# Causal attention on Trainium2: the first scores in a ring of three single PSUM banks, the second scores in a ring of three, and row maxima over one bank

## The chip, the core and the metric

The kernel runs on one NeuronCore of one Trainium2 chip. The metric is the device time in microseconds (us) of one launch of the whole program.

The engines are named as in the profile: PE is TensorE (matmuls; PEld are its weight loads, which overlap them), DVE is VectorE, ACT is ScalarE, POOL is GpSimd, SP is SyncE. The matmul results land in PSUM, which has eight banks of 512 float32 values per partition.

## The reference

The program is a chain of eight layers (four attention-like mixers, four feed-forward ones) over 32 batches of 256 tokens with 128 features. The change touches one of them, the third mixer, a causal attention with 16 heads of 8 features. After low-rank projections it computes, for each batch and head:

```
scores = q @ k.T / sqrt(8)            # 256 x 256, masked to columns <= row
attn   = softmax(scores, axis=-1)
o      = attn @ v                     # 256 x 8
x      = x + concat(o over heads) @ W_o
```

A second attention near the end of the program (no mask, called `h3`) shares its code with this one (`h2`).

## The kernel before

`attend(tag, causal, ...)` emits both attentions. The work goes batch by batch. For a batch the kernel makes two sorts of score:

- **First scores** (queries on partitions), only to find each row's maximum. `late_scores` does the rows 128 to 255 of two heads into one bank (2 matmuls of 256 columns and a mask matmul of 256 columns; L2312, L2314). `early_scores` does the rows 0 to 127 of four heads into one bank (4 of 128 columns and a mask matmul of 512; L2327, L2329). Two banks make a *unit*. A batch has six units, and DVE's `maximum` (L2198) reduces a unit in one instruction of 1024 elements per partition. `ps_1` has four banks, so it holds two units; unit k uses banks 2*(k%2) and the next one.
- **Second scores** (keys on partitions), with the negated maxima as extra rows of q. `scores` does one head into one bank of `ps_2` (256 + 128 columns and a mask matmul of 256; L2355, L2356, L2358). ACT's `weights` (L2449) takes the exponential of the bank into SBUF. `ps_2` has two banks, head h uses bank h%2.

After four heads `weigh` (L2377) multiplies the exponentials with the values: 16 matmuls that use a 128x32 tile of the array each, four side by side. `turn_sums`, `turn_max`, `turn_out` and `project_out` (L2386, L2392, L2399, L2406) turn the sums, the maxima and the output, all through one bank `ps_m`; DVE's `norm` and `added` (L2205, L2209, L2216) and ACT's copies (L2454, L2466, L2472) stand between them. POOL splits the maxima of a batch in three bfloat16 parts (L2244 to L2250) and sends them by DMA into the extra rows of q (L2275).

Everything is software pipelined and the order on each engine is written out by hand in `step`. In step b, PE does for h = 0 to 15: the second scores of head h of batch b, now and then one of the helpers, and then in twelve of the sixteen places (h%8 in 0, 1, 3, 4, 5, 7) one bank of first scores of batch b+2 (`max_scores`). Steps -2 and -1 have first scores alone, steps 30 and 31 second scores alone, and step 32 finishes the last batch. The loop covers the steps 1 to 28.

Buffers are freed by counts. `at(name, b, k)` is "signal `name` has been raised k times in batch b", so `at("ex", b, -1)` means all but the last of the sixteen exponentials of batch b-1. Two waits matter here, both on PE:

```
pe.wait_ge(*at("mx", b, k - 1))       # unit k of first scores: unit k-2 has been reduced
pe.wait_ge(*at("ex", b, h - 1))       # head h of second scores: head h-2 has been exponentiated
```

The second one holds across batches as well: 16 is a multiple of two, so head 0 uses the bank of head 14 before it, and head 1 that of head 15.

Of the kernel before, what the change touches and what calls it, by code (L numbers as in the profile page):

```python
# [19 lines left out]
P = 128  # L20
# [152 lines left out]
def build(nc, x_in, pack_in, maskb_in, w0_in, w1_in, w3_in, out, ktab, ychan, q_stack, k_stack, ones_rows, v_ones,  # L173
          m_parts, xs1, xs3, ys):
    ctx = ExitStack()
    with ctx:
# [11 lines left out]
        def bank(name, stack, n=1):  # L188
            return stack.enter_context(nc.psum_tensor(name, [P, n, 512], F32))
# [99 lines left out]
        for t, nf, choices in (("e1", F1 // P, 2), ("e3", F3 // P, 1)):  # L289
# [25 lines left out]
                ("s1", units), ("mx", units), ("mf", 1), ("ms", 3), ("ml", 1), ("mt", 1), ("mc", 1),   # L315
                ("vp", 2), ("s2", NH), ("ex", NH), ("pv", 4), ("ev", 2), ("tu", 2), ("rec", 2), ("on", 2), ("ot", 1),
                ("otc", 1), ("out", 1), ("x", 1))},
            loaded=[SlotSignal(pool, f"{t}_loaded{u}", 64, u + 4, 4) for u in range(4)]) for t, units in (("h2", 6), ("h3", 8))}
        z_s, z_n, z_g, z_a = sig("z_shifted", 1), sig("z_normed", 1), sig("z_gain", 1), sig("z_done", 1)
        z_d = [SlotSignal(pool, f"z_stored{j}", 16, j, 6) for j in range(6)]  # L320

# [1776 lines left out]
        def attend(tag, causal, dst, w, buffers, load):  # L2098
# [2 lines left out]
            scale = HD ** -0.5  # L2101
            SW = SEQ + P if causal else TPB * SEQ
            UNITS = s["mx"].per

            def at(name, b, k):

                return s[name].now(b, k)
# [6 lines left out]
            with ExitStack() as st:  # L2114
# [11 lines left out]
                oT = sb(f"{tag}_oT", [P, SEQ], stack=st)  # L2126
                identb = sb(f"{tag}_identb", [P, P], BF16, stack=st)
                zero = sb(f"{tag}_zero", [P, 1], stack=st)
                ps_1 = bank(f"{tag}_ps_1", st, 4)
                ps_2 = bank(f"{tag}_ps_2", st, 2)  # L2130
                ps_of = bank(f"{tag}_ps_o", st)
                ps_mf = bank(f"{tag}_ps_m", st)
                ps_o, ps_m = ps_of[:, 0, 0:SEQ], ps_mf[:, 0, 0:SEQ]
# [21 lines left out]
                with pool.loop_block(NB) as block:  # L2155
# [19 lines left out]
                    @block.vector  # L2175
                    def _(dve):
                        for n in range(2):
                            link(dve, dve.memset(vp[n][:, :, :, :], 0.0))
                        link(dve, dve.memset(zero[:, :], 0.0))
                        link(dve, dve.tensor_copy(identb[:, :], ident))  # L2180

                        def maximum(b, u, k):

                            n = u % 2
                            dve.wait_ge(*at("s1", b, k + 1))
                            if k == 0:
                                dve.wait_ge(*at("ml", b, -1))
                            pair = ps_1[:, 2 * (k % 2):2 * (k % 2) + 2, :]
                            if not causal:
                                to, got = nm[n][:, 2 * k:2 * k + 2, :], pair.rearrange("p o (q c) -> p o q c", q=TPB)  # L2190
                            elif k % 3 != 1:
                                h0 = 8 * (k // 3) + HG * (k % 3 // 2)
                                to = nm[n][:, h0:h0 + HG, 1].rearrange("p (o h) -> p o h", o=2)
                                got = pair.rearrange("p o (h c) -> p o h c", c=SEQ)
                            else:
                                to = nm[n][:, 8 * (k // 3):8 * (k // 3) + 8, 0].rearrange("p (o h) -> p o h", o=2)
                                got = pair.rearrange("p o (h c) -> p o h c", c=P)
                            dve.tensor_reduce(to, got, AX, ALU.max, negate=True).then_inc(s["mx"].sem, 1)  # L2198

                        def norm(b, k):  # L2200

                            tv = ps_m.rearrange("p (q h e) -> p q h e", q=TPB, e=16)
                            dve.wait_ge(*at("tu", b, k + 1))
                            dve.wait_ge(*at("on", b, k))
                            dve.reciprocal(rec[:, :, :], tv[:, :, :, HD]).then_inc(s["rec"].sem, 1)  # L2205
                            dve.wait_ge(*at("rec", b, k + 1))
                            if k == 0:
                                dve.wait_ge(*at("ot", b, 0))
                            dve.tensor_tensor(on[:, :, 8 * k:8 * (k + 1), :], tv[:, :, :, 0:HD],  # L2209
                                              rec[:, :, :].unsqueeze(3).to_broadcast([P, TPB, 8, HD]), ALU.mult  # L2210
                                              ).then_inc(s["on"].sem, 1)

                        def added(b):
                            dve.wait_ge(*at("out", b, 1))
                            xd = dst[:, ds(b * TPB, TPB), :]
                            dve.tensor_tensor(xd, xd, ps_m.rearrange("p (t d) -> p t d", t=TPB), ALU.add  # L2216
                                              ).then_inc(s["x"].sem, 1)

                        def step(b, u, r, first, turn, body, tail):
                            for k in range(UNITS):  # L2220
                                if k == 1 and tail:
                                    norm(b - 1, 0)
                                if k == (3 if causal else 4) and tail:
                                    norm(b - 1, 1)
                                if k == UNITS - 1 and tail:
                                    added(b - 1)
                                if first:
                                    maximum(b + 2, u, k)
                            if tail:
                                count(dve, dst, (b - 1) * TPB, TPB, *at("x", b - 1, 1))  # L2230

                        run(dve, step)
# [48 lines left out]
                    def _(pe):  # L2281
# [3 lines left out]
                        def unit_free(b, u, r, k):  # L2285

                            if k == 0 and isinstance(b, int) and b < SLOTS:
                                pe.wait_ge(first_in[tag][u], 48)
                                if b == 2:
                                    pe.wait_ge(first_in[tag][3], 48)  # L2290
                            elif k == 0:
                                pe.wait_ge(*s["loaded"][u].last(r, 64))
                            pe.wait_ge(*at("mx", b, k - 1))

                        def pair_scores(b, u, r, k):

# [6 lines left out]

                        def late_scores(b, u, r, half, part, bank):

                            k = 3 * half + 2 * part
                            if bank == 0:
                                unit_free(b, u, r, k)
                            o = ps_1[:, 2 * (k % 2) + bank, :].rearrange("p (h c) -> p h c", c=SEQ)
                            for j in range(2):  # L2310
                                h = 8 * half + HG * part + 2 * bank + j
                                pe.matmul(o[:, j, :], sq[u][:, h, P:2 * P], sk[u][:, h, :], start=(j == 0), stop=False,  # L2312
                                          skip_group_check=True)
                            ins = pe.matmul(o[:, :, P:2 * P], mskb[:, 0:P], mskb[:, P:2 * P].unsqueeze(1).to_broadcast([P, 2, P]),  # L2314
                                            start=False, stop=True, skip_group_check=True)
                            if bank == 1:
                                ins.then_inc(s["s1"].sem, 1)

                        def early_scores(b, u, r, half, bank):

                            k = 3 * half + 1
                            if bank == 0:
                                unit_free(b, u, r, k)
                            o = ps_1[:, 2 * (k % 2) + bank, :].rearrange("p (h c) -> p h c", c=P)
                            for j in range(HG):
                                h = 8 * half + HG * bank + j
                                pe.matmul(o[:, j, :], sq[u][:, h, 0:P], sk[u][:, h, 0:P], start=(j == 0), stop=False,  # L2327
                                          skip_group_check=True)
                            ins = pe.matmul(o[:, :, :], mskb[:, 0:P], mskb[:, P:2 * P].unsqueeze(1).to_broadcast([P, HG, P]),  # L2329
                                            start=False, stop=True, skip_group_check=True)  # L2330
                            if bank == 1:
                                ins.then_inc(s["s1"].sem, 1)

                        def max_scores(b, u, r, h):

# [12 lines left out]
                        def scores(b, u, h):  # L2348

                            if h == 0:  # L2350
                                maxima_moved(pe, b)
                            pe.wait_ge(*at("ex", b, h - 1))
                            o, hd = ps_2[:, h % 2, :], head(h)
                            if causal:
                                pe.matmul(o[:, 0:SEQ], sk[u][:, hd, 0:P], sq[u][:, hd, :], start=True, stop=False, skip_group_check=True)  # L2355
                                pe.matmul(o[:, SEQ:SW], sk[u][:, hd, P:2 * P], sq[u][:, hd, P:], start=False, stop=False,  # L2356
# [86 lines left out]
                    def _(act):  # L2443
                        def weights(b, h):
                            g, j = h // HG, h % HG
                            act.wait_ge(*at("s2", b, h + 1))
                            if j == 0:
                                act.wait_ge(*at("pv", b, g - 1))
                            act.activation(pt[g % 2][:, j, :], ps_2[:, h % 2, 0:SW], ACT.Exp, scale=scale).then_inc(s["ex"].sem, 1)  # L2449

                        def keep_sums(b, k):
                            act.wait_ge(*at("pv", b, 2 * k + 2))
# [526 lines left out]
```

## Time and profile before

| what | value |
|---|---|
| median of three runs | 3539.38 us (3533.64 to 3543.10) |
| profiled execution, its own time | 3545.52 us |
| span of the profile (first to last instruction) | 3543.7 us |
| mean granted PE clock over the span | 0.863 |
| causal attention stage, from its first reduction's set-up to its last statistics | 1882.5 to 2343.0 us, 460.5 us |
| PE busy in that stage | 452.39 us |
| DVE, ACT, POOL busy in that stage | 287.45, 283.68, 103.34 us |

The profiled execution stands 6.1 us above the median. The stage is 13% of the span. A busy PE in this profile is a PE with a matmul in its pipeline, since the ends of matmuls are modelled; start times tell more: a matmul of 256 columns at full clock is followed by the next one 0.11 us later.

### The profile page before, as it was taken

To read this page: it belongs to the slowest core of one execution; us is meant where nothing else is said; L and a number is where in the kernel's file an instruction comes from. 1 tells how busy PE (TensorE), PEld (TensorE's weight loads), DVE (VectorE), ACT (ScalarE), POOL (GpSimd) and SP (SyncE) were. 2 spreads that over 40 slices of the span, in tenths; PEclk is the share of its full clock that TensorE was granted. 3 is DMA by queue.
4 is the path that set the end of the run, shared out by engine and by line. 5 is a ranking of instruction groups with operands and counts; after the bars stand their busy time and mean duration, and the time that the engine had idled before them with its cause. 6 is when DMAs were issued, how large, how long until landed. Compare 5 with 4: busy or idle time off the path is not lost. (4 is left out here: it accounts for less than half of the span.)

```text
span 3543.7 us, 71949 instructions
## 1 busy us (share of the span) xinstructions
PE 2592.4 (73%) x20194; PEld 1890.8 (53%) x20194; DVE 2241.5 (63%) x4945; ACT 1578.9 (45%) x3615; POOL 725.9 (20%) x1065
## 2 busy tenths in 40 slices
PE   3545858999977666999157999986564999982280
PEld 1333453449966532999135777765332666652260
DVE  5924967238778522676765666646885888865267
ACT  2503612334354232666043666642243777751253
POOL 0000100000000166455301222200221222212553
PEclk7878959999999588999588999978798999985695
DMA  3097100100090111222396555500077565610123
GB/s 95 5 256 178 59 0 14 36 22 0 0 157 26 45 43 43 69 69 65 122 317 75 67 73 72 67 1 1 0 244 149 71 74 72 73 42 20 53 78 101
DMA packets 337603, 261.80 MB, mean 74 GB/s; under 512 B 24988, under 2 KB 319308, under 8 KB 337164
## 3 DMA queue, kind: packets, MB, share of 16 engines
q1 hardware_dynamic: 309720, 223.88, 31.1%
q0 software_dynamic: 19072, 28.28, 2.6%
q10 hardware_dynamic: 8704, 8.39, 0.8%
q8 instruction: 46, 0.75, 0.1%
q14 instruction: 61, 0.50, 0.1%
HBM read 144.03 MB, written 113.29 MB: 73 GB/s over the span
## 5 line engine op out<-in xcount | busy, mean ns | idle before, releaser
L2449 ACT ACTIVATE h_pt<-h_ps 128x384 f32<-128x384 f32 (+1 forms) x1024 | 543.0, 544 | 279.0 <-PE h_ps L2358 143.8
L2198 DVE TENSOR_REDUCE h_nm<-h_ps 128x4 f32<-128x1024 f32 (+1 forms) x448 | 538.9, 1218 | 159.9 <-PE h_ps L2329 64.1
L1607 POOL DMA_INDIRECT sorted_rows<-e_row,e_pos x192 | 184.6, 961 | 439.9 <-DVE e_row L1586 236.1
L1797 POOL DMA_INDIRECT results<-e_y,e_ykey x208 | 211.5, 1017 | 193.4 <-DVE e_y L1786 174.0
L2377 PE MATMUL h_ps_o<-h_pt,h_vp 128*32 128x256 f32 (+1 forms) x4096 | 246.8, 359 | 1.3 <-ACT h_pt L2449 1.3
L1844 ACT ACTIVATE e_hid<-e_ps_h,e_wt 128x128 f32<-128x128 f32 x688 | 202.4, 368 | 20.6 <-PE e_ps_h L1818 14.1
L1818 PE MATMUL e_ps_h<-e_hT,e_wt 128*128 128x128 f32 x1376 | 198.7, 284 | 16.0 <-ACT e_hT L1839 8.2
L1754 DVE TENSOR_SCALAR e_wt<-w 128x1156 f32 (+1 forms) x208 | 139.8, 673 | 98.9 <-DVE e_y L1786 68.9
L2363 PE MATMUL h_ps<-h_sq,h_sk 128*128 128x256 bf16 x1024 | 193.6, 275 | 9.2 <-ACT h_pt L2449 4.4
L1826 PE MATMUL e_ps_o<-e_wt,e_hid 128*128 128x128 f32 x1376 | 195.3, 281 | 4.9 <-ACT e_hid L1844 1.8
L1818 PEld LDWEIGHTS e_ps_h<-e_hT,e_wt 128*128 128x128 f32 x1376 | 175.0, 196 | 29.2 <-issue 17.6
L2300 PE MATMUL h_ps<-h_sk,h_sq 128*128 128x256 bf16 x1024 | 154.9, 275 | 41.6 <-DVE h_identb L2180 34.4
L1826 PEld LDWEIGHTS e_ps_o<-e_wt,e_hid 128*128 128x128 f32 x1376 | 173.1, 194 | 8.7 <-issue 5.4
L2377 PEld LDWEIGHTS h_ps_o<-h_pt,h_vp 128*32 128x32 f32 x4096 | 107.1, 109 | 92.3 <-issue 36.7
L2244 POOL TENSOR_TENSOR h_mpart<-h_nm,h_zero 128x32 bf16<-128x32 f32 x64 | 14.9, 233 | 674.5 <-DVE h_nm L2198 674.5
L1811 PE MATMUL e_ps_t<-pack,e_xt 128*128 128x128 f32 x208 | 58.6, 284 | 121.4 <-DMA e_xt<-sorted_rows 121.2
L2355 PE MATMUL h_ps<-h_sq,h_sk 128*128 128x256 bf16 x512 | 140.5, 274 | 2.1 <-ACT h_pt L2449 1.7
L2358 PE MATMUL h_ps<-h_mskb 128*128 128x256 bf16 x512 | 139.6, 273 | 0.0
L1141 DVE TENSOR_TENSOR x_hid<-x_gelu,x_ps_u 128x512 f32<-128x512 f32 x64 | 43.3, 687 | 141.9 <-ACT x_gelu L1126 141.9
L2312 PE MATMUL h_ps<-h_sk,h_sq 128*128 128x256 bf16 x512 | 99.3, 277 | 45.6 <-DVE h_identb L2180 44.5
L2300 PEld LDWEIGHTS h_ps<-h_sk,h_sq 128*128 128x128 bf16 x1024 | 99.1, 98 | 57.4 <-DVE h_identb L2180 34.6
L2363 PEld LDWEIGHTS h_ps<-h_sq,h_sk 128*128 128x128 bf16 x1024 | 83.7, 98 | 71.7 <-ACT h_pt L2449 62.0
(436 smaller groups left out, 6261.0 us busy)
## 6 DMA issues: line engine op xcount, KB each, us to landing
h_sq<-q_stack SPq DMA_DIRECT2D x64, 384.0 KB
h_sk<-k_stack SPq DMA_DIRECT2D x64, 384.0 KB
sorted_rows<-pad SPq DMA_DIRECT2D x26, 520.0 KB, 10.7
e_xt<-sorted_rows SPq DMA_DIRECT2D x104, 130.0 KB
e_got<-results SPq DMA_DIRECT2D x24, 512.0 KB, 6.3
q_stack<-p_parts SPq DMA_DIRECT2D x32, 384.0 KB
k_stack<-p_parts SPq DMA_DIRECT2D x32, 384.0 KB
v_ones<-p_v SPq DMA_DIRECT2D x32, 288.0 KB, 2.7
```

What stands on the lines that cost most here:

```text
L1607: gp.indirect_dma_start(xs[:, :], bass.IndirectOffsetOnAxis(ap=pos[:, n % choices, tile:tile + 1], axis=0), row[n % ROWS][:, :], None).the ...
L1754: dve.tensor_scalar(wt[j % 4][:, :], w[:, :, :].rearrange("p e w -> p (e w)")[:, ds(at, wc)], 1.0, None, ALU.mult).then_inc(e_w.sem, 1)
L1797: gp.indirect_dma_start(ys[:, :], bass.IndirectOffsetOnAxis(ap=key[m // 4][:, m % 4:m % 4 + 1], axis=0), y[m][:, :], None).then_inc(return ...
L1818: pe.matmul(ps_h[:, k, 0:P], wt[j % 4][:, f * P:(f + 1) * P], hT[j % 4][:, :], start=True, stop=True).then_inc(e_h.sem, 1)
L1826: ins = pe.matmul(o, hid_t[m][:, f, :], wt[m][:, f_dim + f * D:f_dim + (f + 1) * D], start=(f == 0), stop=(f == nf - 1))
L1844: act.activation(hid_t[j % 4][:, f, :], ps_h[:, (j * nf + f) % 4, 0:P], func, bias=wt[j % 4][:, o_b1 + f:o_b1 + f + 1]).then_inc(e_a.sem, 1)
L2198: dve.tensor_reduce(to, got, AX, ALU.max, negate=True).then_inc(s["mx"].sem, 1)
L2300: ins = pe.matmul(ps_1[:, h % 4, q * SEQ:(q + 1) * SEQ], sq[u][:, h, q * P:(q + 1) * P], sk[u][:, h, :], start=True, stop=True)
L2355: pe.matmul(o[:, 0:SEQ], sk[u][:, hd, 0:P], sq[u][:, hd, :], start=True, stop=False, skip_group_check=True)
L2363: ins = pe.matmul(o[:, t * SEQ:(t + 1) * SEQ], sk[u][:, hd, t * P:(t + 1) * P], sq[u][:, hd, :], start=True, stop=True)
L2377: ins = pe.matmul(ps_o[32 * j:32 * (j + 1), q0:], vp[u % 2][:, t, head(HG * g + j), :], pt[g % 2][:, j, t * SEQ:(t + 1) * SEQ - q0], start ...
L2449: act.activation(pt[g % 2][:, j, :], ps_2[:, h % 2, 0:SW], ACT.Exp, scale=scale).then_inc(s["ex"].sem, 1)
```

## The change

The causal attention gets other rings. (The attention without a mask keeps its four and two banks and its waits.)

- `ps_1` becomes a ring of three single banks. A unit is now one bank: twelve units in a batch, each with its own wait and its own signal. Unit k waits until unit k-3 has been reduced.
- DVE reduces each bank by itself: twelve instructions of 512 elements in place of six of 1024. `norm` and `added` stand at the same places between them.
- `ps_2` becomes a ring of three banks, head h uses bank h%3. Head h waits until head h-3 has been exponentiated. As 16 is not a multiple of three, the first three heads of a batch have counts of their own: head 0 falls on the bank of head 15 of the batch before (15%3 = 0), head 1 on that of head 13, head 2 on that of head 14.

```
+            RING = 3 if causal else 2
...
-                ps_1 = bank(f"{tag}_ps_1", st, 4)
-                ps_2 = bank(f"{tag}_ps_2", st, 2)
+                ps_1 = bank(f"{tag}_ps_1", st, 3 if causal else 4)
+                ps_2 = bank(f"{tag}_ps_2", st, RING)
...
# DVE, maximum
-            elif k % 3 != 1:
-                h0 = 8 * (k // 3) + HG * (k % 3 // 2)
-                to = nm[n][:, h0:h0 + HG, 1].rearrange("p (o h) -> p o h", o=2)
-                got = pair.rearrange("p o (h c) -> p o h c", c=SEQ)
             else:
-                to = nm[n][:, 8 * (k // 3):8 * (k // 3) + 8, 0].rearrange("p (o h) -> p o h", o=2)
-                got = pair.rearrange("p o (h c) -> p o h c", c=P)
+                half, i = divmod(k, UNITS // 2)
+                part, o = divmod(i, 2)
+                if part != 1:
+                    h0, n_h, q = 8 * half + HG * (part // 2) + 2 * o, 2, 1
+                else:
+                    h0, n_h, q = 8 * half + HG * o, HG, 0
+                to, got = nm[n][:, h0:h0 + n_h, q], ps_1[:, k % RING, :].rearrange("p (h c) -> p h c", h=n_h)
             dve.tensor_reduce(to, got, AX, ALU.max, negate=True).then_inc(s["mx"].sem, 1)
...
# DVE, step: the same places among twice as many units
-                                if k == 1 and tail:
+                                if k == (2 if causal else 1) and tail:
                                     norm(b - 1, 0)
-                                if k == (3 if causal else 4) and tail:
+                                if k == (6 if causal else 4) and tail:
                                     norm(b - 1, 1)
...
# PE, unit_free
-                            pe.wait_ge(*at("mx", b, k - 1))
+                            pe.wait_ge(*at("mx", b, k + 1 - RING))
...
# PE, late_scores (early_scores alike)
-                            k = 3 * half + 2 * part
-                            if bank == 0:
-                                unit_free(b, u, r, k)
-                            o = ps_1[:, 2 * (k % 2) + bank, :].rearrange("p (h c) -> p h c", c=SEQ)
+                            k = 6 * half + 4 * part + bank
+                            unit_free(b, u, r, k)
+                            o = ps_1[:, k % RING, :].rearrange("p (h c) -> p h c", c=SEQ)
...
# PE, scores
-                            pe.wait_ge(*at("ex", b, h - 1))
-                            o, hd = ps_2[:, h % 2, :], head(h)
+                            pe.wait_ge(*at("ex", b, h + 1 - RING if h >= RING or not causal else (0, -2, -1)[h]))
+                            o, hd = ps_2[:, h % RING, :], head(h)
```

The order of the matmuls on PE stays as it was; what moves is where PE waits. Here is PE at the seam between two batches, before the change: head 15 of batch b (L2355 to L2358), a bank of first scores (L2312, L2314), and head 0 of batch b+1. `signal20` counts exponentials, `signal9` reduced units.

```order
L2355 MATMUL h_ps<-h_sq,h_sk 128x256 [waits signal20]
L2356 MATMUL h_ps<-h_sq,h_sk 128x128
L2358 MATMUL h_ps<-h_mskb 128x2x128
L2312 MATMUL h_ps<-h_sk,h_sq 128x256 x2
L2314 MATMUL h_ps<-h_mskb 128x2x128
L2149 ISA
L2352 ISA [waits h2_maxima_in]
L2355 MATMUL h_ps<-h_sq,h_sk 128x256 [waits signal20]
```

The same place in the changed kernel (L2351 to L2354 are the second scores there, L2313 and L2315 the first):

```order
L2351 MATMUL h_ps<-h_sq,h_sk 128x256 [waits signal20]
L2352 MATMUL h_ps<-h_sq,h_sk 128x128
L2354 MATMUL h_ps<-h_mskb 128x2x128
L2295 REGISTER_ALU
L2313 MATMUL h_ps<-h_sk,h_sq 128x256 [waits signal9]
L2313 MATMUL h_ps<-h_sk,h_sq 128x256
L2315 MATMUL h_ps<-h_mskb 128x2x128
L2150 ISA
L2348 ISA [waits h2_maxima_in]
L2351 MATMUL h_ps<-h_sq,h_sk 128x256 [waits signal20]
```

The matmuls stand as before. The second bank of a pair has gained a register instruction and a wait of its own (six of these in a batch), and the last row's wait on the exponentials now asks for all sixteen of the batch before, where it asked for fifteen.

On DVE, one step of the stage (29, the last with first scores) before the change. L2198 are the reductions, L2205 and L2209 `norm`, L2216 `added`.

```order
L2198 TENSOR_REDUCE h_nm<-h_ps 128x4
L2205 RECIPROCAL h_rec<-h_ps_m 128x16
L2209 TENSOR_TENSOR h_on<-h_ps_m,h_rec 128x2x64
L2198 TENSOR_REDUCE h_nm<-h_ps 128x8
L2198 TENSOR_REDUCE h_nm<-h_ps 128x4
L2205 RECIPROCAL h_rec<-h_ps_m 128x16
L2209 TENSOR_TENSOR h_on<-h_ps_m,h_rec 128x2x64
L2198 TENSOR_REDUCE h_nm<-h_ps 128x4
L2198 TENSOR_REDUCE h_nm<-h_ps 128x8
L2216 TENSOR_TENSOR x_res<-x_res,h_ps_m 128x256
L2198 TENSOR_REDUCE h_nm<-h_ps 128x4
```

The same step after it (L2200 are the reductions, L2207, L2211 and L2218 the others):

```order
L2200 TENSOR_REDUCE h_nm<-h_ps 128x2 x2
L2207 RECIPROCAL h_rec<-h_ps_m 128x16
L2211 TENSOR_TENSOR h_on<-h_ps_m,h_rec 128x2x64
L2200 TENSOR_REDUCE h_nm<-h_ps 128x4 x2
L2200 TENSOR_REDUCE h_nm<-h_ps 128x2 x2
L2207 RECIPROCAL h_rec<-h_ps_m 128x16
L2211 TENSOR_TENSOR h_on<-h_ps_m,h_rec 128x2x64
L2200 TENSOR_REDUCE h_nm<-h_ps 128x2 x2
L2200 TENSOR_REDUCE h_nm<-h_ps 128x4 x2
L2200 TENSOR_REDUCE h_nm<-h_ps 128x2
L2218 TENSOR_TENSOR x_res<-x_res,h_ps_m 128x256
L2200 TENSOR_REDUCE h_nm<-h_ps 128x2
```

Each reduction has become two, except that `added` now stands between the two halves of the last pair.

## Rows read from the trace of the kernel before

**Rows 1.** Busy time by stretch (us, then each engine's busy time and instruction count).

```profile
core 0: us, PE busy (x) PEld busy (x) DVE busy (x) ACT busy (x) POOL busy (x), PEclk, DMA share, GB/s
1882.50:2343.00 460.50, 452.39 (x5376) 334.59 (x5376) 287.45 (x419) 283.68 (x641) 103.34 (x288) 0.99 0.51 62
...
1950.00:2300.00 350.00, 350.00 (x4233) 263.26 (x4232) 224.96 (x328) 222.99 (x503) 80.64 (x225) 1.00 0.58 70
...
1952.12:1966.02 13.90, 13.90 (x170) 10.45 (x168) 8.95 (x14) 8.87 (x21) 3.23 (x9) 1.00 0.58 73
1966.02:1979.92 13.90, 13.90 (x170) 10.46 (x168) 8.95 (x14) 8.87 (x21) 3.23 (x9) 1.00 0.58 71
```

**Rows 2.** Waits on PEld, 1950 to 2300 us: total, times, longest.

```profile
PEld h_ps L2355 <- ACT h_pt L2449: 9.9, 50, 0.2
PEld h_ps_o L2377 <- issue: 8.0, 51, 0.2
PEld h_ps_o L2377 <- ACT h_pt L2449: 7.9, 50, 0.2
PEld h_ps_m L2406 <- issue: 5.2, 26, 0.2
PEld h_ps_m L2386 <- issue: 4.9, 25, 0.2
```

**Rows 3.** Timeline of the seam between two batches (start, length, engine, line).

```profile
2104.42 0.27 PE L2355 MATMUL h_ps<-h_sq,h_sk 128*128 128x256 bf16 x1
...
2104.59 0.27 PE L2358 MATMUL h_ps<-h_mskb 128*128 128x256 bf16 x1
...
2104.69 0.38 PE L2312 MATMUL h_ps<-h_sk,h_sq 128*128 128x256 bf16 x2
...
2104.89 0.49 ACT L2449 ACTIVATE h_pt<-h_ps 128x384 f32<-128x384 f32 x1 [1.21 <-PE h_ps L2358]
2104.91 0.27 PE L2314 MATMUL h_ps<-h_mskb 128*128 128x256 bf16 x1
...
2105.02 0.27 PE L2355 MATMUL h_ps<-h_sq,h_sk 128*128 128x256 bf16 x1
...
2105.18 0.27 PE L2358 MATMUL h_ps<-h_mskb 128*128 128x256 bf16 x1
...
2105.30 0.38 PE L2312 MATMUL h_ps<-h_sk,h_sq 128*128 128x256 bf16 x2
...
2299.62 0.27 PE L2355 MATMUL h_ps<-h_sq,h_sk 128*128 128x256 bf16 x1
```

**Rows 4.** Timeline near the stage's end: a true wait of PE on an exponential.

```profile
2316.45 0.49 ACT L2449 ACTIVATE h_pt<-h_ps 128x384 f32<-128x384 f32 x1 [0.94 <-PE h_ps L2358]
...
2317.00 0.28 PE L2355 MATMUL h_ps<-h_sq,h_sk 128*128 128x256 bf16 x1 [0.31 <-ACT h_pt L2449]
```

**Rows 5.** Groups by line and shape on DVE, 1870 to 2370 us.

```profile
L2198 DVE TENSOR_REDUCE h_nm<-h_ps 128x4 f32<-128x1024 f32 x128 | 155.6, 1217 | 49.9 <-PE h_ps L2314 47.5
...
L2209 DVE TENSOR_TENSOR h_on<-h_ps_m,h_rec 128x128 f32<-128x128 f32 x64 | 18.6, 291 | 2.8
...
L2216 DVE TENSOR_TENSOR x_res<-x_res,h_ps_m 128x256 f32<-128x256 f32 x4 | 1.7, 422 | 12.0 <-PE h_ps_m L2406 12.0
```

**Rows 6.** Timelines of the stage's start: DVE's reductions, then PE.

```profile
1886.30 2.51 DVE L2198 TENSOR_REDUCE h_nm<-h_ps 128x8 f32<-128x1024 f32 x2 [0.42 <-PE h_ps L2329]
1889.04 4.62 DVE L2198 TENSOR_REDUCE h_nm<-h_ps 128x4 f32<-128x1024 f32 x4 [0.24 <-PE h_ps L2314]
...
1897.44 0.39 PE L2312 MATMUL h_ps<-h_sk,h_sq 128*128 128x256 bf16 x2
...
1898.10 0.27 PE L2355 MATMUL h_ps<-h_sq,h_sk 128*128 128x256 bf16 x1
```

**Rows 7.** Timeline of PE at the seam 30 to 31 and in step 31.

```profile
2324.97 0.27 PE L2358 MATMUL h_ps<-h_mskb 128*128 128x256 bf16 x1
2325.08 0.27 PE L2355 MATMUL h_ps<-h_sq,h_sk 128*128 128x256 bf16 x1
...
2325.83 0.28 PE L2355 MATMUL h_ps<-h_sq,h_sk 128*128 128x256 bf16 x1 [0.31 <-ACT h_pt L2449]
...
2326.59 0.86 PE L2377 MATMUL h_ps_o<-h_pt,h_vp 128*32 128x256 f32 x16
2327.38 0.44 PE L2386 MATMUL h_ps_m<-pack,h_sums 128*128 128x128 f32 x2
```

**Rows 8.** Waits, 2313.4 to 2325.1 us, then 2325.0 to 2336.6 us.

```profile
PEld h_ps L2355 <- ACT h_pt L2449: 2.9, 10, 0.5
...
PEld h_ps L2355 <- ACT h_pt L2449: 3.3, 10, 0.5
```

More of the change, by code:

```diff
@@ L317, in build @@
                 ("otc", 1), ("out", 1), ("x", 1))},
-            loaded=[SlotSignal(pool, f"{t}_loaded{u}", 64, u + 4, 4) for u in range(4)]) for t, units in (("h2", 6), ("h3", 8))}
+            loaded=[SlotSignal(pool, f"{t}_loaded{u}", 64, u + 4, 4) for u in range(4)]) for t, units in (("h2", 12), ("h3", 8))}
         z_s, z_n, z_g, z_a = sig("z_shifted", 1), sig("z_normed", 1), sig("z_gain", 1), sig("z_done", 1)
@@ L2187, in maximum @@
                                 dve.wait_ge(*at("ml", b, -1))
-                            pair = ps_1[:, 2 * (k % 2):2 * (k % 2) + 2, :]
                             if not causal:
+                                pair = ps_1[:, 2 * (k % 2):2 * (k % 2) + 2, :]
                                 to, got = nm[n][:, 2 * k:2 * k + 2, :], pair.rearrange("p o (q c) -> p o q c", q=TPB)
-                            elif k % 3 != 1:
-                                h0 = 8 * (k // 3) + HG * (k % 3 // 2)
-                                to = nm[n][:, h0:h0 + HG, 1].rearrange("p (o h) -> p o h", o=2)
-                                got = pair.rearrange("p o (h c) -> p o h c", c=SEQ)
-                            else:
-                                to = nm[n][:, 8 * (k // 3):8 * (k // 3) + 8, 0].rearrange("p (o h) -> p o h", o=2)
-                                got = pair.rearrange("p o (h c) -> p o h c", c=P)
+                            else:
+                                half, i = divmod(k, UNITS // 2)
[5 more added lines that the diff above has]
+                                to, got = nm[n][:, h0:h0 + n_h, q], ps_1[:, k % RING, :].rearrange("p (h c) -> p h c", h=n_h)
                             dve.tensor_reduce(to, got, AX, ALU.max, negate=True).then_inc(s["mx"].sem, 1)
@@ L2313, in late_scores @@
                                           skip_group_check=True)
[L2314 to L2317, printed above, removed]
+                            pe.matmul(o[:, :, P:2 * P], mskb[:, 0:P], mskb[:, P:2 * P].unsqueeze(1).to_broadcast([P, 2, P]),
+                                      start=False, stop=True, skip_group_check=True).then_inc(s["s1"].sem, 1)
                         def early_scores(b, u, r, half, bank):
[L2321 to L2324, printed above, removed]
+                            k = 6 * half + 2 + bank
+                            unit_free(b, u, r, k)
+                            o = ps_1[:, k % RING, :].rearrange("p (h c) -> p h c", c=P)
                             for j in range(HG):
@@ L2328, in early_scores @@
                                           skip_group_check=True)
[L2329 to L2332, printed above, removed]
+                            pe.matmul(o[:, :, :], mskb[:, 0:P], mskb[:, P:2 * P].unsqueeze(1).to_broadcast([P, HG, P]),
+                                      start=False, stop=True, skip_group_check=True).then_inc(s["s1"].sem, 1)
                         def max_scores(b, u, r, h):
@@ L2448, in weights @@
                                 act.wait_ge(*at("pv", b, g - 1))
-                            act.activation(pt[g % 2][:, j, :], ps_2[:, h % 2, 0:SW], ACT.Exp, scale=scale).then_inc(s["ex"].sem, 1)
+                            act.activation(pt[g % 2][:, j, :], ps_2[:, h % RING, 0:SW], ACT.Exp, scale=scale).then_inc(s["ex"].sem, 1)
                         def keep_sums(b, k):
```

## The prediction

> **What bounds the kernel now.** I read the busy time by stretch first. In the causal attention, PE has a matmul in flight for 452 of 460.5 us, and for all of the 350 us in its middle, at full granted clock; DVE and ACT are busy for about 64% there [rows 1]. Two successive batches take 13.90 us each with the same counts and the same busy times [rows 1], and the pattern holds: head 0 of a batch starts at 1952.12, eleven batches of 13.90 later at 2105.02, and another fourteen later at 2299.62 [rows 1, 3]. So the stage runs as one fixed pattern that PE sets.
>
> The question is whether PE ever waits for a buffer in this pattern. The list of waits shows only gaps of at most 0.2 us before weight loads [rows 2]. One kind looks like what a deeper ring would cure: L2355, after a `weigh`, "released by ACT", 50 times, 9.9 us. But the same 0.2 stands in front of L2406 and L2386 after a `weigh` under "issue" (0.20 each: 5.2 us in 26, 4.9 in 25), and these read nothing that an exponential frees [rows 2]. A gap that is the same whoever follows belongs to the change from the 128x32 tiles to the full array, not to a buffer. So I take it that in the steady pattern PE never waits for `mx` or `ex`: the rings as they stand are deep enough, and a deeper one can give nothing there. PE waits on them only at the two ends of the stage, where the pattern is not complete.
>
> **The change, part by part.**
>
> *The seam between batches: a wait that was not there.* Head 0 now needs the bank of head 15, the head just before it. The timeline of a seam [rows 3]: the last matmul of head 15 starts at 2104.59, ACT takes its exponential from 2104.89 to 2105.38, and PE starts head 0 at 2105.02, with one bank of first scores (0.33 us) between. With the new count PE must stand until 2105.38 and the signal's way. That way is seen where PE truly waits today: an exponential ends at 2316.45 + 0.49 = 2316.94, the matmul starts at 2317.00, 0.06 later [rows 4]. Head 0 then starts at 2105.44 in place of 2105.02: **0.42 us**. ACT has no backlog there (it had been idle for 1.21 us before this exponential [rows 3]), so the wait is not longer. It is not shorter either: the start of head 15 hangs on PE's own order. Nothing covers it, as PE is the bound and works in order: everything behind head 0, the first scores of batch b+2 and the next `weigh` among it, moves back by as much. Nothing later gives it back, since PE has no idle time to shrink. The seams from 0/1 to 29/30 have this shape, 30 of them: 30 x 0.42 = **+12.6 us**. The pattern would take 14.32 us.
>
> *Heads 1 and 2* wait for heads 13 and 14 of the batch before: both are done when head 15 is, so nothing is added. Heads 3 to 15 wait for one head earlier than before: no wait today, none then.
>
> *Two waits and signals for one, twice the reductions.* Six more register instructions and waits per batch on PE. A bank of first scores that stands today without a wait starts at 2104.69, 0.10 after the matmul before it (2104.59); one with register work and a wait starts at 2105.30, 0.12 after 2105.18 [rows 3]. Both are the 0.11 of a 256-column stream, so a wait that is fulfilled costs nothing: **0**. It is hidden by the matmul that runs; if it weren't, see the third rival.
>
> A reduction of 512 elements is in no row. From below it is half of 1.22 us, 0.61; from above the whole 1.22. Two other DVE operations that read PSUM cost 0.291 at 128 and 0.422 at 256 columns [rows 5], 1.02 ns a column, so 1.217 - 512 x 0.00102 = 0.69 us, which I take. Its start-to-start pitch is shorter: four in a row took 4.62, so (4.62 - 1.22) / 3 = 1.13, which is 0.09 below the duration [rows 6]; 0.60 for the new one. In the steady pattern DVE's load goes from 8.95 to about 8.95 + 6 x 0.17 = 10.0 us of 14.3. A bank is due for its next unit four places of h later, which leaves over three heads' time, some 2.5 us, against 0.69: no wait. Its last reduction of a batch comes earlier than now, so POOL's chain and the maxima's DMA have no less slack than they had.
>
> The Trainium skill (VectorE: DVE Perf Modes, the table in the section on the TRN2 errata) gives a PSUM source 120 cycles and one per element. By that 512 elements take 632 cycles, 0.66 us, and 1024 take 1.19; the trace has 1.22, so the rows decide, and the sum would change by less than half a microsecond in the ramp below.
>
> *The ramp at the start.* Steps -2 and -1 have only first scores, and DVE sets their pace: head 0 of batch 0 starts at 1898.10, right behind the last unit of batch 1 (1897.44) [rows 6], which had waited for a reduction. Today, that is nine units of 1.13 to 1.2 us behind the one at 1886.30. With single banks the last unit waits for reduction 21 of 24. While PE is still cold DVE is fed no faster than now; I put reduction 9 at about 1889.4, and then 12 at a pitch of 0.60 and one of 0.69 give 1897.3, and head 0 at 1897.7. With a pitch of 0.69 it is 1898.8. So between -0.4 and +0.7; the first head's next two units then wait less than the 0.23 us or so that they do now. I take **-0.4**, with -0.8 to +0.9 as ends. (The maxima of batch 0 must have come by DMA too; they are there shortly before 1898.)
>
> *The end.* Steps 30 and 31 have no first scores, a head takes 0.27 us of PE, an exponential 0.49, and there PE does wait. A head that waits is seen by its distance: 2325.08 to 2325.83 is 0.75 where 0.27 would do, so 0.48 [rows 7]. The waits of L2355's weight loads come to 2.9 us in step 30 and 3.3 in step 31 [rows 8]; less 0.2 for each of the three or four that only follow a `weigh`, and counted at the matmuls' starts, head by head, that is 1.95 and 2.4. The third bank lets PE run one head further ahead, and the `weigh` every fourth head (0.79, 2326.59 to 2327.38 [rows 7]) lets ACT catch up, so nearly all of it goes: -1.95 and -2.2 (the last exponential still has to be waited for). The seam 30/31 gets a wait of its own: head 15's last matmul at 2324.97, its exponential 0.31 later and 0.49 long, and 0.06, so 2325.83 in place of 2325.08: +0.75. Together **-3.4**.
>
> **Sum:** 12.6 + 0 - 0.4 - 3.4 = **+8.8 us**. The stage ends later by that, and the next one starts behind it. The profiled execution, 3545.5 us, becomes 3554.3; the median of the runs is 6.1 lower, 3539.4, and becomes **3548.2**.
>
> **The rivals.**
>
> 1. *The 0.2 us before L2355 is a wait for a PSUM bank and goes.* This is the one that ends on the other side. Price: 9.9 us in 25 batches is 0.40 a batch, times 30 is -11.9, so -3.1 in all, 3536. It decides if more than 0.3 of the 0.42 at each seam comes back. Against it: the same gap before L2406 and L2386 [rows 2]. The Trainium skill has a rule for each reading. Perfetto Trace Analysis (Identifying the Most-Contended Engine) says that the same gap repeating on the engine that should be saturated can mean too few SBUF or PSUM buffers; this would make the change pay. TensorEngine Tiling (Key Properties) says that changing the tiling mode drains the engine; this would leave the gaps. The trace agrees with the second.
> 2. *The reduction has more fixed cost than I think.* If one of 512 took the full 1.22, DVE would need 12 x 1.13 + 1.9 = 15.5 us a batch, 1.2 above the 14.3, and the ramp would grow by some 8: about +50, 3590. It decides from about 1.03 us a reduction. Against it: the slope in [rows 5].
> 3. *PE pays for the six added waits.* No row shows it. As a price, 0.09 us each, which is what the 0.2 of [rows 2] has above the stream's 0.11: 6 x 0.09 x 32 = +17, 3565. Against it: the two equal distances in [rows 3].
> 4. *The seam's wait isn't felt*, because head 0 is not on the path, or the pattern shifts to hide it: then -3.8, 3536. Against it: PE in order, always busy [rows 1].
>
> **How the numbers follow.** The forecast has 0.68, the first rival 0.10, the second 0.03, the third 0.12, the fourth 0.07. A measurement of this kernel can tell about 0.3% from no change, 10.6 us. The forecast's +8.8 lies just inside, and the runs before scatter by 5 us around their median, so of its 0.68 I give 0.25 to slower, 0.42 to same, 0.01 to faster. Rivals 1 and 4 (-3 to -4) give 0.12 to same and 0.05 to faster, 2 and 3 all to slower, 0.15, less 0.03 for the third if it is partial. Faster 0.06, same 0.57, slower 0.37. The forecast's own range is 3543 to 3554; for 8 in 10 it must reach to rivals 1 and 4 below and partly to the third above: 3536 to 3561.
>
> **What the new profile would show.** Right: a fixed pattern of 14.32 us; at each seam a row of L2351 with an idle time ended by ACT, 0.42 us later than the stream would have it, and nothing else changed on PE; 0.2 us gaps after each `weigh` as before; the reductions 384 at 0.69 us; head 0 of batch 0 at 15.0 us from the first matmul, less 0.4; steps 30 and 31 with hardly a wait but that at the seam. Wrong: a pattern of 13.90 (fourth rival), one of 13.9 with smaller gaps after `weigh` (first), waits of L2313 or L2325 on DVE in the middle (second), more than 0.11 us between matmuls at a new wait (third).

## The result, and the profile after

The changed kernel takes 3546.26 us (median of 8 runs, 3543.20 to 3551.77), against 3538.13 us for the kernel before, which was run beside it (8 runs). The ratio is 1.0026 with a 95% interval of 1.0015 to 1.0037: slower by 8 us, a difference that is surely there and is smaller than the 0.3% that I had called the limit of no change. The forecast was 3548.2, 8.8 us above before.

The page of the profiled execution after the change, its span and the busy times:

```profile
span 3545.8 us, 72477 instructions
## 1 busy us (share of the span) xinstructions
PE 2598.4 (73%) x20194; PEld 1890.5 (53%) x20194; DVE 2267.2 (64%) x5137; ACT 1578.1 (45%) x3615; POOL 728.6 (21%) x1065
```

The spans of the two profiled executions differ by only 2.1 us, since the stages ahead of the causal attention happened to be 6.6 us shorter in this one (its first matmul starts at 1876.49 us, that of before at 1883.09) and those behind it 0.5. So I compare the stage itself, from its first matmul to its last statistics: 460.0 us before, 469.3 after, +9.2.

The middle of the stage, in the view by stretch. The first two rows are two successive batches:

```profile
core 0: us, PE busy (x) PEld busy (x) DVE busy (x) ACT busy (x) POOL busy (x), PEclk, DMA share, GB/s
1917.46:1931.79 14.33, 14.07 (x168) 10.39 (x168) 9.75 (x19) 8.89 (x21) 3.29 (x9) 1.00 0.56 71
1931.79:1946.12 14.33, 14.07 (x168) 10.39 (x168) 9.75 (x19) 8.89 (x21) 3.29 (x9) 1.00 0.56 70
```

PE was busy 13.90 of 13.90 us [rows 1]; now it is busy 14.07 of 14.33. The pattern has grown by 0.43 us. Where, the waits of PE between 1950 and 2290 us say: there is one kind, one per batch.

```profile
PE h_ps L2351 <- ACT h_pt L2445: 5.9, 23, 0.3
```

And the seam itself, which answers to [rows 3]:

```profile
2103.15 0.27 PE L2354 MATMUL h_ps<-h_mskb 128*128 128x256 bf16 x1
...
2103.46 0.49 ACT L2445 ACTIVATE h_pt<-h_ps 128x384 f32<-128x384 f32 x1 [1.21 <-PE h_ps L2354]
2103.48 0.27 PE L2315 MATMUL h_ps<-h_mskb 128*128 128x256 bf16 x1
...
2104.00 0.10 PEld L2351 LDWEIGHTS h_ps<-h_sq,h_sk 128*128 128x128 bf16 x1 [0.53 <-ACT h_pt L2445]
2104.01 0.28 PE L2351 MATMUL h_ps<-h_sq,h_sk 128*128 128x256 bf16 x1 [0.26 <-ACT h_pt L2445]
```

Head 15's exponential runs from 2103.46 to 2103.95, and head 0 starts at 2104.01, 0.06 later; without the wait it would have started 0.11 after 2103.48, at 2103.59. The distance is 0.42. The idle time that the row prints, 0.26, is less, because the end of a matmul is modelled to lie 0.16 behind the point at which the next one could start. Whoever reads the printed idle time alone sees 5.9 us for the 23 seams of this window, where 23 x 0.42 is 9.7, and misses nearly four tenths of the cost.

The reductions, which were in no row before, are in the groups now:

```profile
L2200 DVE TENSOR_REDUCE h_nm<-h_ps 128x2 f32<-128x512 f32 x256 | 169.8, 687 | 45.1 <-PE h_ps L2315 42.2
...
L2200 DVE TENSOR_REDUCE h_nm<-h_ps 128x4 f32<-128x512 f32 x128 | 88.2, 691 | 37.0 <-PE h_ps L2327 34.5
```

### The profile page after: what moved, and what is told of

It reads as the page before. It is cut to its first block and busy times, and to the rows that moved or that the text cites. A ratio compares the mean times of both kernels' runs of the same rounds, so it can differ in the third digit from the quotient of the medians.

```text
span 3545.8 us, 72477 instructions
## 1 busy us (share of the span) xinstructions
PE 2598.4 (73%) x20194; PEld 1890.5 (53%) x20194; DVE 2267.2 (64%) x5137; ACT 1578.1 (45%) x3615; POOL 728.6 (21%) x1065
## 5 line engine op out<-in xcount | busy, mean ns | idle before, releaser
L2200 DVE TENSOR_REDUCE h_nm<-h_ps 128x4 f32<-128x1024 f32 (+2 forms) x640 | 560.6, 900 | 128.1 <-PE h_ps L2302 42.5
L2351 PE MATMUL h_ps<-h_sq,h_sk 128*128 128x256 bf16 x512 | 140.5, 274 | 8.5 <-ACT h_pt L2445 8.5
L2354 PE MATMUL h_ps<-h_mskb 128*128 128x256 bf16 x512 | 139.5, 273 | 0.0
L2313 PE MATMUL h_ps<-h_sk,h_sq 128*128 128x256 bf16 x512 | 99.6, 277 | 44.8 <-DVE h_identb L2181 44.4
L2277 POOL DMA_DIRECT2D h_sq<-h_mT x192 | 95.2, 500 | 133.6 <-ACT h_mT L2462 133.1
```

## Experiments

Every kernel was timed beside the kernel before on its own chip, and the chips differ by over 1%, so ratios are compared (the first four share one chip and its 27 runs of the kernel before). "Pattern" is the distance between the starts of head 0 in successive batches, in the middle of the stage.

**The added wait alone.** The kernel before, with one count changed:

```
-                            pe.wait_ge(*at("ex", b, h - 1))
+                            pe.wait_ge(*at("ex", b, 0 if causal and h == 0 else h - 1))
```

> The kernel before with one thing added: head 0 of a batch waits for all sixteen exponentials of the batch before, which its bank (that of head 14) does not need. Rings, reductions and everything else stay. Theory (the seam's wait is the whole cost): a pattern of 14.32 to 14.33 us in place of 13.90, each seam 0.42 later, +13 us in all (31 seams; nothing is given back at the ends). Rival (the cost comes from six more waits and twice the reductions): 13.90 and no change, since none of that is in it.

Measured: 1.0044 (1.0030 to 1.0058), 3515.07 against 3499.74 us. Its stage takes 473.6 us, 13.6 more than before's. The timeline of two seams ten batches apart:

```profile
2020.96 0.27 PE L2358 MATMUL h_ps<-h_mskb 128*128 128x256 bf16 x1
...
2021.27 0.49 ACT L2449 ACTIVATE h_pt<-h_ps 128x384 f32<-128x384 f32 x1 [1.21 <-PE h_ps L2358]
...
2021.82 0.28 PE L2355 MATMUL h_ps<-h_sq,h_sk 128*128 128x256 bf16 x1 [0.26 <-ACT h_pt L2449]
...
2165.12 0.28 PE L2355 MATMUL h_ps<-h_sq,h_sk 128*128 128x256 bf16 x1 [0.26 <-ACT h_pt L2449]
```

(2165.12 - 2021.82) / 10 = 14.33: the whole new pattern, from one wait, with the old rings and the old reductions. The rival's 13.90 is out.

**The first ring alone.** The changed kernel with `ps_2` put back:

```
-                ps_2 = bank(f"{tag}_ps_2", st, RING)
+                ps_2 = bank(f"{tag}_ps_2", st, 2)
...
-                            pe.wait_ge(*at("ex", b, h + 1 - RING if h >= RING or not causal else (0, -2, -1)[h]))
-                            o, hd = ps_2[:, h % RING, :], head(h)
+                            pe.wait_ge(*at("ex", b, h - 1))
+                            o, hd = ps_2[:, h % 2, :], head(h)
... # and h % 2 in place of h % RING where ACT reads the bank
```

> The first half of the change alone: ps_1 a ring of three single banks with twelve reductions of 512 elements a batch, twelve waits and twelve signals; ps_2 stays at two banks with its old waits. Theory: pattern 13.90, reductions at 0.69 us, the ramp about 1.1 us shorter as in the changed kernel, the end as before: -1 us, not to be told from no change. Rival (the added waits and reductions cost PE time): a pattern above 13.90, by 0.09 for each of six waits 14.4 us, +17 us.

Measured: 0.9993 (0.9984 to 1.0002). Two seams ten batches apart:

```profile
2018.12 0.27 PE L2351 MATMUL h_ps<-h_sq,h_sk 128*128 128x256 bf16 x1
...
2157.12 0.27 PE L2351 MATMUL h_ps<-h_sq,h_sk 128*128 128x256 bf16 x1
```

13.90 again, with six more waits and six more reductions in every batch. They cost PE nothing, and the start-up is 0.8 us shorter (27.33 us before, 26.54 here, from the first matmul to head 0 of batch 1), of which the next batch, with 14.05, gives 0.15 back. A part of the 0.8 is not the ring's: full clock was granted 4.4 us after the stage's first matmul here, 5.7 us after it in the profile of before.

**Another place for head 15.** Three banks, but the sixteenth head goes to bank 1:

```
+            PLACE = [h % RING for h in range(NH)]
+            if causal:
+                PLACE[NH - 1] = 1
...
-                            pe.wait_ge(*at("ex", b, h + 1 - RING if h >= RING or not causal else (0, -2, -1)[h]))
-                            o, hd = ps_2[:, h % RING, :], head(h)
+                            pe.wait_ge(*at("ex", b, h - 1 if not causal else {0: -3, 1: 0, 2: -1, NH - 1: NH - 2}.get(h, h - 2)))
+                            o, hd = ps_2[:, PLACE[h], :], head(h)
... # and PLACE[h] in place of h % RING where ACT reads the bank
```

> The changed kernel with one bank number and four counts changed: head 15 goes to bank 1 in place of bank 0. So head 15 waits for head 13, head 0 for head 12, head 1 for head 15, head 2 for head 14; all other heads keep a distance of three. In the kernel before, head 15 started 1.34 us after the end of exponential 13, and head 1 starts 0.24 us after that of exponential 15, so neither should wait. Theory: pattern 13.90 again, the ramp 1.1 shorter, the waits of the last two steps mostly gone (-4), so -4 to -5 us against before, 3534. Rival (something else in the third bank costs): the pattern stays above 13.90 and the time at or above that of before. If head 1 does wait, the pattern is a little above 13.90.

Measured: 0.9986 (0.9977 to 0.9995), 3495.59 against 3499.74 us. It has the lowest ratio here: faster than before by 4 us (the interval allows 2 to 8), within the 4 to 5 expected, and, by the ratios, 0.4% faster than the changed kernel. The seam, and one ten batches on:

```profile
2010.78 0.27 PE L2357 MATMUL h_ps<-h_mskb 128*128 128x256 bf16 x1
...
2011.08 0.49 ACT L2448 ACTIVATE h_pt<-h_ps 128x384 f32<-128x384 f32 x1 [1.21 <-PE h_ps L2357]
2011.10 0.27 PE L2318 MATMUL h_ps<-h_mskb 128*128 128x256 bf16 x1
2011.21 0.27 PE L2354 MATMUL h_ps<-h_sq,h_sk 128*128 128x256 bf16 x1
...
2150.21 0.27 PE L2354 MATMUL h_ps<-h_sq,h_sk 128*128 128x256 bf16 x1
```

Head 0 starts 0.11 after the matmul before it, while the exponential of head 15 still runs. 13.90, so neither head 1 nor head 15 waits. The third bank as such costs nothing; its whole cost in the change was where the ring closed over the batch's end, and what it gains at the two ends of the stage is kept.

**More work in front of the wait.** The changed kernel, where the first bank of first scores of a step comes ahead of head 0:

```
+                                if first and causal and h == 0:
+                                    max_scores(b + 2, *later, h)
                                 if body:
                                     scores(b, u, h)
...
-                                if first:
+                                if first and not (causal and h == 0):
                                     max_scores(b + 2, *later, h)
```

> The changed kernel with one step moved on PE: in each step the first bank of first scores (0.33 us) comes ahead of the second scores of head 0, not behind them. The wait for exponential 15 stays, but has two banks of first scores in front of it. Theory (the wait costs what is not covered): 0.42 - 0.33 = 0.1 us a seam, a pattern of 13.99 to 14.0, so +3 for the seams and -1 to -5 for the ends: no change against before within 3 us. Rival (the wait's cost is not a matter of cover, for instance a fixed price of a new dependence): the pattern stays at 14.33 and the time at +8.

Measured: 0.9995 (0.9986 to 1.0004). The seam, and one ten batches on:

```profile
2016.38 0.49 ACT L2447 ACTIVATE h_pt<-h_ps 128x384 f32<-128x384 f32 x1 [1.21 <-PE h_ps L2354]
...
2016.72 0.27 PE L2315 MATMUL h_ps<-h_mskb 128*128 128x256 bf16 x1
2016.92 0.28 PE L2351 MATMUL h_ps<-h_sq,h_sk 128*128 128x256 bf16 x1
...
2156.95 0.28 PE L2351 MATMUL h_ps<-h_sq,h_sk 128*128 128x256 bf16 x1
```

14.00: the dependence is the same as in the changed kernel, and it costs 0.10 in place of 0.43. What counts is the part of the way over ACT that PE's own work doesn't cover. Note that the row of head 0 prints no idle time at all here, though the pattern shows 0.1 of it.

**A second wait of the same kind.** The changed kernel, with head 8 too waiting for the head just before it:

```
-                            pe.wait_ge(*at("ex", b, h + 1 - RING if h >= RING or not causal else (0, -2, -1)[h]))
+                            pe.wait_ge(*at("ex", b, h if causal and h == 8 else h + 1 - RING if h >= RING or not causal else (0, -2, -1)[h]))
```

> The changed kernel with the disputed wait doubled: head 8 too waits for the exponential of the head just before it (head 7), with one bank of first scores between, as at the seam. Theory: 0.42 us more in each of 32 batches, pattern 14.75, +13 us against the changed kernel, +21 against before. Rival (PE's time comes back elsewhere in the pattern, ACT having slack): less than that, down to the +8 of the changed kernel.

Measured: 1.0062 (1.0048 to 1.0075), 3518.30 against 3498.79 us, +19.5 where +21 was expected. The seam, head 8 half a batch on, and the seam ten batches on:

```profile
2022.17 0.28 PE L2351 MATMUL h_ps<-h_sq,h_sk 128*128 128x256 bf16 x1 [0.26 <-ACT h_pt L2445]
...
2029.36 0.28 PE L2351 MATMUL h_ps<-h_sq,h_sk 128*128 128x256 bf16 x1 [0.26 <-ACT h_pt L2445]
...
2169.77 0.28 PE L2351 MATMUL h_ps<-h_sq,h_sk 128*128 128x256 bf16 x1 [0.25 <-ACT h_pt L2445]
```

14.76, another 0.43 on the 14.33. The price is paid in full each time; nothing comes back.

**Each weigh cut in two.** This one is on the step that ruled out the first rival: whether the 0.2 us around a `weigh` belong to the change of tiles. The kernel before, with the last eight matmuls of each `weigh` one head later:

```
-                                if j == 2:
+                                if j == 2 or (j == 3 and causal):
+                                    parts = range(j - 2, j - 1) if causal else range(TPB)
                                     if g and body:
-                                        weigh(b, u, g - 1)
+                                        weigh(b, u, g - 1, parts)
... # and the same for the last weigh of the batch before; inside weigh the loop runs over parts,
... # the waits stand before the first half alone, the signal behind the second
```

> The kernel before with each weigh of the causal attention cut in two: its first eight matmuls stay behind the second scores of the third head of a group, its last eight go behind those of the fourth head. The same matmuls and the same buffers; PE goes over to the 128x32 tiles eight times a batch in place of four. The reading that the 0.2 us gaps before and after a weigh belong to the change of tiles: each added pair costs 0.09 going in (0.20 where the stream has 0.11) and 0.11 coming out, 4 x 0.2 = 0.8 us a batch, a pattern of about 14.7 and +25 us or a little more. The reading that the gap behind a weigh is a wait for an exponential to free a bank: L2355 comes no earlier behind the exponentials than it did, so there is nothing to add, and half a weigh leaves ACT less to catch up with: a pattern of 13.9 to 14.1.

Measured: 1.0086 (1.0065 to 1.0107), 3579.19 against 3545.89 us, and a pattern of 14.92. The timeline of the two halves of one `weigh`:

```profile
2052.77 0.27 PE L2358 MATMUL h_ps<-h_mskb 128*128 128x256 bf16 x1
2052.98 0.64 PE L2378 MATMUL h_ps_o<-h_pt,h_vp 128*32 128x256 f32 x8
2053.55 0.28 PE L2355 MATMUL h_ps<-h_sq,h_sk 128*128 128x256 bf16 x1
2053.67 0.22 PE L2356 MATMUL h_ps<-h_sq,h_sk 128*128 128x128 bf16 x1
2053.72 0.27 PE L2358 MATMUL h_ps<-h_mskb 128*128 128x256 bf16 x1
2053.93 0.43 PE L2378 MATMUL h_ps_o<-h_pt,h_vp 128*32 128x128 f32 x8
2054.28 0.44 PE L2401 MATMUL h_ps_m<-pack,h_on 128*128 128x128 f32 x2
```

From start to next start the halves take 0.57 and 0.35, together 0.92, where the whole took 0.79 (2326.59 to 2327.38 [rows 7]); and each half has 0.21 in front of it in place of 0.11 (2052.77 to 2052.98, 2053.72 to 2053.93). So a further change of tiles costs 0.13 + 0.10 = 0.23 us, four times a batch 0.9 of the 1.02 measured. The remaining 0.1 lies in the first matmul behind each added change: L2401's is followed by the next bank of first scores after 0.28 (2054.28 to 2054.56), where L2388, which has the same two fp32 matmuls but no `weigh` in front, takes 0.22 (2051.46 to 2051.68), and each of the three others costs 0.01 more than elsewhere. The expectation had been 0.8. The other reading is out: the matmuls and the banks are the same, and the gap stands in front of L2401 too, which reads no exponential.

A `weigh` differs from its neighbours in type as well (fp32 beside bf16). That is not what costs. The same trace has fp32 matmuls over the full array behind bf16 ones, 0.11 apart as in any stream, and bf16 matmuls on a 128x48 tile, which have the 0.20 in front of them:

```profile
2051.35 0.27 PE L2358 MATMUL h_ps<-h_mskb 128*128 128x256 bf16 x1
2051.46 0.38 PE L2388 MATMUL h_ps_m<-pack,h_sums 128*128 128x128 f32 x2
...
2063.33 0.27 PE L2358 MATMUL h_ps<-h_mskb 128*128 128x256 bf16 x1
2063.53 0.29 PE L2394 MATMUL h_ps_m<-h_identb,h_mpart 128*48 128x128 bf16 x2
```

## Why the prediction held

The mechanism was the one that was forecast, and its three terms can be read off the trace one by one. That their sum comes within 0.4 us of the forecast is partly luck: the seams and the end came out 0.4 dearer each, and the start-up, 0.5 cheaper, took one of the two back.

| term | forecast | measured in the stage |
|---|---|---|
| the pattern | 14.32 us | 14.33 us |
| 30 seams | +12.6 | +13.05 |
| start-up | -0.4 | -0.9 |
| the last two steps | -3.4 | -3.0 |
| sum | +8.8 | +9.2 |
| medians of the program | +8.8 | +8.1 |

- **The seam.** 0.42 a seam was forecast from four rows. In the loop it is 0.43. At the three seams behind the loop it is 0.09 more: 0.51 and 0.52 at the first two (14.41 and 14.42 in place of 14.33), 0.84 in place of 0.75 at the last, which has no first scores in front of it. This is the one thing here that no row of before could have told; it is explained below. The wait alone makes the whole new pattern, a second such wait makes it again, more cover takes it away as forecast, and another bank for head 15 removes it.
- **Six waits and six reductions for nothing.** Held: with the first ring alone the pattern stays at 13.90. A reduction of 512 elements takes 0.687 to 0.691 us in the mean; 0.69 had been taken from the slope of two other operations. DVE is busy for 9.75 us of a batch, not 10.0: the forecast had left out that reductions back to back overlap (two take 1.28 or 1.29, not 1.38). An estimate from the table in the Trainium skill, VectorE: DVE Perf Modes (The TRN2 errata), would have been 0.66 us; the trace decides.
- **The start-up.** The pitch of the reductions came out at 0.60 as worked out from [rows 6]. Head 0 of batch 0 starts 14.6 us after the first matmul, 15.0 before: the -0.4 of the forecast. This figure moves with the moment at which full clock is granted, 4.4 to 5.9 us after the first matmul in these profiles: it is 14.8 to 15.05 in the three profiles with the old first ring and 14.5 to 14.6 in four with the new one (the kernel with more cover has another order there), so the gain is between 0.2 and 0.5. The other half of the gain lies just behind it, in the first steps of batch 0, where PE had waited for a reduction for 0.23 us and for its second bank; I had named it and given it nothing.
- **The end.** The term was 0.4 too large. The waits went, a little more of them than I had counted, but two things were added. The wait at the last seam was 0.84, not 0.75, and the last `project_out` ran at half the clock:

```profile
2343.54 1.22 PE L2402 MATMUL h_ps_m<-pack,h_oT 128*128 128x128 f32 x4 [0.47 <-ACT h_oT L2468]
```

  And in the kernel before:

```profile
2341.42 0.71 PE L2406 MATMUL h_ps_m<-pack,h_oT 128*128 128x128 f32 x4 [0.47 <-ACT h_oT L2472]
```

  The granted clock of that stretch is 0.50 (the 1.2 GHz level), and 1.00 in the same place before. Ahead of it PE had done four short pieces with waits between, as before too. The clock falls near this matmul in both: at 2343.2 here, 0.3 before its start, and at 2342.8 in the kernel before, 1.4 after it. The kernels with head 15 on bank 1 and with the second seam show the same 1.22, the four others 0.71. So this half microsecond hangs on which side of the fall the last `project_out` lands. It belongs to no ring, and no row of before told on which side it would be.
- **The rivals.** The first (the 0.2 us gaps are a shortage of banks) was put down at 0.10; with a third bank the gap behind a `weigh` is unchanged, 0.79 from the start of the `weigh` to that of the head behind it (1940.61 to 1941.40, and 2113.57 to 2114.36 before), and cutting each `weigh` in two doubles their number. First the changed kernel:

```profile
1940.61 0.86 PE L2373 MATMUL h_ps_o<-h_pt,h_vp 128*32 128x256 f32 x16
1941.40 0.28 PE L2351 MATMUL h_ps<-h_sq,h_sk 128*128 128x256 bf16 x1
```

  And the kernel before, whose trace could have settled it alone:

```profile
2113.07 1.09 ACT L2449 ACTIVATE h_pt<-h_ps 128x384 f32<-128x384 f32 x2 [0.25 <-PE h_ps L2358]
2113.57 0.86 PE L2377 MATMUL h_ps_o<-h_pt,h_vp 128*32 128x256 f32 x16
2114.36 0.28 PE L2355 MATMUL h_ps<-h_sq,h_sk 128*128 128x256 bf16 x1
```

  Here head 11 starts 0.8 after the end of exponential 9, whose bank it takes (the first of the two in the ACT row, it ends at 2113.56). No head in the middle of that stage starts less than 0.16 behind the exponential that it needs, where a true wait shows 0.06. The Trainium skill has a rule for each reading. That of Perfetto Trace Analysis (in its section Optimization Strategy, not the one before it that the prediction names), that a gap which repeats can mean too few buffers, does not fit here. That of TensorEngine Tiling (Array Packing) (Key Properties), that changing the tiling mode drains the engine, fits: the same gap stands at each such change, whoever comes next. The second (a dear reduction) fell with 0.69, the third (dear waits) with the pattern of 13.90, the fourth (no cost at the seam) with 14.33.

What I would not claim: the changed kernel's own share of noise. 8.1 us between the medians and 9.2 in the stage agree within the interval (5 to 13 us), no closer.

## What to carry to other kernels

Before a ring is deepened, look whether the bound engine waits on it at all; here the list of waits showed only gaps that were the same whoever followed, and a deeper ring had nothing to take but the waits at the two ends of the stage, some 4 us. Then write down, for each buffer, the distance to its next use over the whole cycle, the loop's seam included: a ring of three under sixteen heads is a ring of one at one place, and that place sets the price. A dependence costs the bound engine its round trip over the other engine less the work that stands between, so either move work there or give the odd item the bank whose distance is two.

## What I had not expected

- A wait that is truly waited for costs more or less by where it sits. In the loop the count of exponentials is carried by the weight load itself, and PE starts 0.06 us after the exponential's end (2103.95 to 2104.01). Behind the loop the same wait stands in a semaphore instruction of its own ahead of the weight load, as the load carries the wait for the maxima's DMA there (the trace has this instruction, of L2348, at 2304.61, 0.04 after the exponential, and the load at 2304.68), and PE starts 0.14 after it:

```profile
2304.08 0.49 ACT L2445 ACTIVATE h_pt<-h_ps 128x384 f32<-128x384 f32 x1 [1.21 <-PE h_ps L2354]
...
2304.71 0.27 PE L2351 MATMUL h_ps<-h_sq,h_sk 128*128 128x256 bf16 x1 [0.34 <-ACT h_pt L2445]
```

  If this holds elsewhere, the later of two waits should be the one on the instruction itself. The 0.09 us is read from these rows and from the three seams; no kernel was made to test it.
- A change from the full array to a 128x32 tile and back costs PE 0.23 us (0.25 with what the matmul behind it loses), also between matmuls that wait for nothing. At four a batch in 32 batches I estimate some 30 us for this kernel, more than all that these rings are worth.
